# Second layer of a feature-crossing kernel: four more weight tiles as split products, first-layer products moved from VectorE to GpSimd, replicated x1 read from PSUM

## The reference, cut to what matters

```python
def _cin_layer(h, h0, W, b):            # W: (128, Hn*32)
    Wr = W.reshape(128, h.shape[1], 32)
    x = jnp.einsum('bhd,bmd,ohm->bod', h, h0, Wr) + b[None, :, None]
    return relu(x)
x1 = _cin_layer(e, e, W1, b1)           # 32 x 32 products per (b, d)
x2 = _cin_layer(x1[:, :64], e, W2, b2)  # 64 x 32 products per (b, d)
z = sum over d of concat([x1[:, 64:], x2], axis=1)
y = relu(relu(concat([z, dense_ctx]) @ W_top1 + b_top1) @ W_top2 + b_top2) @ W_top3
```

## Time and profile before

| | |
|---|---|
| median of 3 runs | 2141.46 us (2140.15 to 2145.08) |
| the profiled execution's own time | 2145.8 us |
| its span in the trace | 2144.1 us |
| busy in the span: TensorE, VectorE, ScalarE, GpSimd | 98%, 96%, 60%, 54% |
| TensorE clock granted | 0.997 of full speed |
| first product of the second layer on TensorE | at 54.69 us |

### The profile page before, as it was taken

The page is one execution under the profiler, slowest core; times in us unless marked ns, Lnnn a source line. Parts: engine busy times, 40 slices in busy tenths (PEclk is TensorE's granted clock), DMA queues, the critical chain, the costliest instruction groups (busy, mean ns, idle before and its releaser), DMA issues.

```text
span 2144.1 us, 27590 instructions
## 1 busy us (share of the span) xinstructions
PE 2103.7 (98%) x6378; PEld 1204.2 (56%) x6378; DVE 2054.1 (96%) x668; ACT 1285.4 (60%) x4499; POOL 1160.0 (54%) x456
## 2 busy tenths in 40 slices
PE   3999999999999999999999999999999999999999
PEld 1555555555555556555555556555555555555554
DVE  5999999999999999999999999999999999999991
ACT  2565665665665665665665665665665665666653
POOL 4666766666766666677676666666766700000000
PEclk9999999999999999999999999999999999999999
DMA  5676676676676776776776776776676776666650
GB/s 180 192 201 195 193 204 193 198 202 194 202 198 193 205 197 192 204 199 191 204 200 190 205 197 191 205 200 190 199 203 190 202 194 176 186 191 176 184 148 0
DMA packets 226937, 405.59 MB, mean 189 GB/s; under 512 B 33377, under 2 KB 33889, under 8 KB 226802
## 3 DMA queue, kind: packets, MB, share of 16 engines
q1 hardware_dynamic: 212594, 380.32, 61.7%
q0 software_dynamic: 14336, 25.19, 4.6%
HBM read 321.49 MB, written 16.78 MB: 158 GB/s over the span
## 4 chain that ended last, share of the span: by engine, by line
PE 94%; DVE 3%; DMA 2%; issue 1%; SPq 0%; POOL 0%; ACT 0%; DVEq 0%; POOLq 0%; ACTq 0%
PE acc L459 40%; PE acc L453 20%; PE acc L467 10%; PE acc L466 10%; PE acc L471 10%; PE acc L454 1%; DVE pfar L390 1%; DVE pnear L390 1%; DMA x1rep<-x 1%; PE acc L511 0%; PE tp L511 0%; DMA near<-emb_rows 0%; DMA rem_b<-emb_rows 0%; POOL gathered L215 0%; SPq L240 0%
## 5 line engine op out<-in xcount | busy, mean ns | idle before, releaser
L215 POOL DMA_INDIRECT gathered<-in_tables,idx x256 | 933.5, 3646 | 112.4 <-issue 58.5
L459 PE MATMUL acc<-pfar,w2T 128*128 128x512 f32 x2048 | 904.8, 595 | 10.6 <-DVE pfar L390 10.6
L567 ACT CAST phi<-pnear 128x4096 fp32r<-128x4096 f32 x128 | 463.4, 3620 | 541.2 <-DVE pnear L390 301.1
L459 PEld LDWEIGHTS acc<-pfar,w2T 128*128 128x128 f32 x2048 | 389.0, 191 | 481.8 <-issue 468.8
L527 ACT ACTIVATE acc<-acc,bias 128x64 f32<-128x64 f32 (+1 forms) x2048 | 579.7, 286 | 18.8 <-PE acc L471 12.2
L390 DVE TENSOR_TENSOR pnear<-near,x1rep 128x4096 f32<-128x4096 f32 x128 | 566.4, 4425 | 21.0 <-DMA x1rep<-x 17.5
L407 DVE TENSOR_TENSOR plo<-pnear,phi 128x4096 fp32r<-128x4096 f32 x128 | 565.5, 4418 | 0.5 <-ACT phi L567 0.5
L390 DVE TENSOR_TENSOR pfar<-far,x1rep 128x4096 f32<-128x4096 f32 x128 | 565.5, 4418 | 0.0
L453 PE MATMUL acc<-prod,w1T 128*128 128x512 f32 x1024 | 464.9, 597 | 14.7 <-DVE rem_parts L380 12.4
L466 PE MATMUL acc<-phi,w2lo 128*128 128x512 f32 x1024 | 452.8, 442 | 0.0
L527 ACT ACTIVATION_READ_ACCUMULATOR acc<-acc,bias (+2 forms) x2048 | 423.8, 207 | 1.5
(11 more groups left out here) (63 smaller groups left out, 282.8 us busy)
## 6 DMA issues: line engine op xcount, KB each, us to landing
near<-emb_rows SPq DMA_DIRECT2D x512, 256.0 KB, 3.8
far<-emb_rows SPq DMA_DIRECT2D x512, 256.0 KB, 4.4
x1rep<-x SPq DMA_DIRECT2D x256, 256.0 KB, 4.2
h<-emb_rows SPq DMA_DIRECT2D x128, 256.0 KB, 3.2
emb_rows<-gathered POOLq DMA_DIRECT2D x128, 128.0 KB, 3.8
gathered<-in_tables,idx POOLq DMA_INDIRECT x256, 6.5
rem_a<-emb_rows SPq DMA_DIRECT2D x64, 64.0 KB, 3.4
rem_b<-emb_rows SPq DMA_DIRECT2D x64, 64.0 KB, 3.3
```

The source lines that it names most:

```text
L215: nc.gpsimd.indirect_dma_start(out=gathered[:, g, :], out_offset=None, in_=a["tables"], in_offset=bass.IndirectOffsetOnAxis(ap=idx[:, g:g ...
L459: mm = nc.tensor.matmul(acc2[s][:, :], w2T[:, t, :], pfar[:, t // K2, t % K2, :], start=(t == 0), stop=False)
L567: nc.scalar.copy(phi[:, :, :], pnear[:, :, :, :].rearrange("p a k n -> p (a k) n")).then_inc(hi_ready, 1)
```

## The change

- VectorE's products read x1 from PSUM: the replication DMA still writes `x1rep` (now one buffer in SBUF), and ScalarE copies it into `x1p` (two PSUM buffers of 1024 columns).
- `prod1`, `rem_prod` and the remainder's low part move to GpSimd, except those of the start. `prod1` is made for chunk c+2 in step c, so the first layer runs two chunks ahead. `near` gets a third buffer.
- 12 of the 16 second-layer tiles are split: the 8 near ones and the first half of the far ones. 4 stay whole.
- The stores of gathered rows move from GpSimd's queue to SyncE's, with three buffers of `gathered` and `idx`. Two gathers are started in each step.
- The rounding and the low part of the four new split tiles are operations of their own (`phi` and `plo` have 12 tiles).
- The order on TensorE is: high products of the near tiles, first layer of chunk c+2, whole products, low products, high products of the four far tiles.
- The loop has six chunks a turn (19 turns), with 6 written out ahead and 8 behind.

```diff
-x1rep = [sb(f"x1rep_{s}", [P, A2, N]) for s in range(2)]
+x1rep = sb("x1rep", [P, A2, N])
+x1p = [ps(f"x1p_{s}", [P, A2 * N]) for s in range(2)]
 GpSimd, step c:
+                if not odd and within(at, 2):
+                    pool.wait_ge(rem_in, 32 * pair + 64)
+                    pool.wait_ge(rem_lo_ready, pair + 1)
+                    nc.gpsimd.tensor_tensor(rem_prod[:, :], rem_a[:, :], rem_b[:, :], ALU.mult).then_inc(rem_prod_ready, 1)
+                if within(at, 2):
+                    pool.wait_ge(acc1_ready, c + 2)
+                    pool.wait_ge(near_in[(u + 2) % 3], LOADS * (turn * (U // 3)) + LOADS * ((u + 2) // 3 + 1))
+                    nc.gpsimd.tensor_tensor(prod1[:, :, :], near[(u + 2) % 3][:, :, :],
+                                            h0[odd][:, :].unsqueeze(1).to_broadcast([P, K1, N]), ALU.mult
+                                            ).then_inc(p1_ready, 1)
+                if not odd and within(at, 2):
+                    pool.wait_ge(rem_hi_ready, pair + 2)
+                    pool.wait_ge(p1_ready, c + 3)
+                    nc.gpsimd.tensor_tensor(rem_parts[2 * REM:3 * REM, :], rem_prod[:, :], ...).then_inc(rem_lo_ready, 1)
+                    pool.wait_ge(rem_lo_ready, pair + 2)
+                if within(at, 7 - odd):
+                    if not odd:
+                        pool.wait_ge(emb_stored, STORES * pair + STORES)
+                        place_idx(pair + 3, u // 2)
+                    for g in range(2 * odd, 2 * odd + 2):
+                        gather(g, u // 2)
 VectorE, step c:
+                dve.wait_ge(x1p_ready, c + 1)
+                products2(pnear[:, :, :, :], near[u % 3][:, :, :], odd, K1).then_inc(pnear_ready, 1)
+                    dve.wait_ge(lo_far_ready, c)
+                    dve.wait_ge(far_used, c)
+                products2(pfar[:, :, :, :], far[odd][:, :, :], odd, K2).then_inc(pfar_ready, 1)
+                dve.wait_ge(hi_near_ready, c + 1)
+                low(slice(0, T_NEAR), pnear[:, :, :, :]).then_inc(lo_near_ready, 1)
+                dve.wait_ge(hi_far_ready, c + 1)
+                low(slice(T_NEAR, T_SPLIT), pfar[:, 0:1, :, :]).then_inc(lo_far_ready, 1)
 TensorE, step c:
+                pe.wait_ge(hi_near_ready, c + 1)
+                high(odd, range(0, T_NEAR)).then_inc(hi_near_used, 1)
+                    pe.wait_ge(p1_ready, c + 3)
+                    layer1(odd)
+                pe.wait_ge(pfar_ready, c + 1)
+                whole(odd).then_inc(far_used, 1)
+                pe.wait_ge(lo_near_ready, c + 1)
+                low(odd, range(0, T_NEAR))
+                pe.wait_ge(lo_far_ready, c + 1)
+                low(odd, range(T_NEAR, T_SPLIT)).then_inc(lo_used, 1)
+                pe.wait_ge(hi_far_ready, c + 1)
+                high(odd, range(T_NEAR, T_SPLIT)).then_inc(acc2_ready, 1)
 SyncE, step c: replicate_x1 (waits x1_ready, x1p_ready), load_rem of c+3 in odd steps,
   load_near of c+3 (waits pnear_ready, p1_ready), load_far of c+2, store_rows in even steps
 ScalarE, step c: hidden1 of c+1, remainder_hi in even steps, phi of the near tiles,
   copy of x1rep to x1p for c+1, phi of the four far tiles, direct2 of c-1, direct1 of c+1
```

More of the change, by code:

```diff
@@ L189, in software_pipeline, with within, begun @@
         def software_pipeline(eng, step):
[L190 to L196, removed]
+            for c in range(U):
+                step(c, 0, c, c)
+            turns = CHUNKS // U - 1
+            with eng.Fori(1, turns) as turn:
+                for u in range(U):
+                    step(turn * U + u, turn, u, None)
+            for c in range(turns * U, CHUNKS):
+                step(c, c // U, c % U, c)
+        def within(at, ahead):
+            return at is None or at + ahead < CHUNKS
+        def begun(at):
+            return at is None or at > 0
         block = ctx.enter_context(nc.Block())
@@ L391, in products2 @@
                     out, h0part.unsqueeze(1).to_broadcast([P, A2, k, N]),
[L392 to L412, removed]
-                    done = products1(pair + 1, s)
-                    if s == 0:
-                        done = remainder_lo(pair + 1)
-                    done.then_inc(p1_ready, 1)
@@ L474, in _, with high @@
-            pe.wait_ge(p1_ready, 1)
-            layer1(0)
-            def step(c, pair, s, first, last):
-                if not (first and s == 0):
-                    layer2_near(c - 1, 1 - s)
-                if not (last and s == 1):
-                    pe.wait_ge(p1_ready, c + 2)
-                    if not (first and s == 0):
-                        pe.wait_ge(z1_ready, c)
-                    layer1(1 - s)
-                if not first:
-                    pe.wait_ge(z2_ready, c - 1)
-                pe.wait_ge(pfar_ready, c + 1)
-                layer2_far(s)
+            def high(s, parts):
+                for t in parts:
+                    nc.tensor.matmul(acc2[s][:, :], w2lo[:, t, :], phi[:, t, :], start=(t == 0), stop=False)
+                    mm = nc.tensor.matmul(acc2[s][:, :], w2hi[:, t, :], phi[:, t, :], start=False, stop=(t == T_SPLIT - 1))
+                return mm
@@ new lines, in low, with whole @@
+            def low(s, parts):
+                for t in parts:
+                    mm = nc.tensor.matmul(acc2[s][:, :], w2hi[:, t, :], plo[:, t, :], start=False, stop=False)
+                return mm
+            def whole(s):
+                for k in range(K2):
+                    mm = nc.tensor.matmul(acc2[s][:, :], w2T[:, k, :], pfar[:, 1, k, :], start=False, stop=False)
+                return mm
+            pe.wait_ge(rem_lo_ready, 1)
+            for c in range(2):
+                pe.wait_ge(p1_ready, c + 1)
+                layer1(c)
@@ L560, in _, with copy_x1rep @@
             direct1(0, 0)
[L562 to L579 removed]
+            def copy_x1rep(s):
+                nc.scalar.copy(x1p[s][:, :], x1rep[:, :, :].rearrange("p a n -> p (a n)")).then_inc(x1p_ready, 1)
```

268 lines of the change are left out of this document (154 added, 114 removed).

## The result

The changed kernel takes 2060.12 us (median of 4 runs, 2058.09 to 2060.97) against 2140.81 for the kernel before (2139.52 to 2145.08; the table ahead of the prediction has three of these four runs). The ratio is 0.9619, with a 95% interval of 0.9607 to 0.9631. The forecast was 2060.

What follows compares the result with a forecast made beforehand. TensorE was taken to set the pace, VectorE about 0.1 us a chunk behind. (16.04 - 15.42) x 128 = 79 us, and 3 at the end, gave 2064; the median's 4.3 us less gave 2060 us, range 2044 to 2126.

Steps and rivals of the forecast that it cites:

- The main term: TensorE in the loop: four tiles go from whole to fp32r passes, 0.68 us less a chunk, 15.36 in place of 16.04.
- the collision: GpSimd's rem_prod in odd steps reaches 0.4 to 1.3 us into the place of VectorE's near low part.
- VectorE's 15.3: VectorE per chunk: loses prod1 and the remainder (2.97 us), gains a low part (2.3), PSUM operands costing next to nothing.
- the 5.1 that I took: GpSimd's two-input product of 2048 elements: bounds 1.7 to 5.1 us, the upper one taken.
- The third rival: PSUM operands don't free the port for GpSimd products, VectorE is held: 21.7 us a chunk, 2865 us; chance 0.08.
- The fourth rival: GpSimd itself becomes the bound, its gathers shut out as often as before: 15.9 us a chunk, 2120 us; chance 0.06.
- The charge of 0.06 us a chunk: Added to TensorE's 15.36 us for rem_prod meeting VectorE's low part, between 0 and 0.14.
- the self-correction: A late VectorE makes TensorE wait, so GpSimd starts at the early end and rem_prod reaches less into the low part.
- The fifth rival: The longer loop costs a code fetch of 4.2 us at each of 19 branches: 80 us, 2140 us; chance 0.05.
- The end: From last pnear to tower: 19.7 us in place of 23.1, a gain of 3 us.
- The start: Same first loads, ScalarE's copy (about 1 us) added before the first product: nothing either way.
- My schedule: Timing in a chunk: if TensorE waits for VectorE, the first layer ends and prod1 may start at 0, with pnear.

Runs made afterwards that it cites:

- without the collision: Changed kernel with rem_prod made on GpSimd ahead of the gathers and its load issued ahead of the replication of x1: 2055.2 us, ratio 0.9596.
- the kernel with the tiny rem_prod: Changed kernel with rem_prod on GpSimd made for one column of 512 only, in the loop: 2056.4 us, ratio 0.9604.

## Why the prediction was right

*The pace.* The main term is shown. The forecast floor of 15.36 us for TensorE is the measured pace of 15.358 (15.353 without the collision), a whole pass and an fp32r pass cost what the earlier trace rows gave, and adding three passes back gives 16.040, against 16.046 for the kernel before. VectorE's 15.3 is 15.20: reading x1 from PSUM costs nothing (4.41 us), and the new low part 2.20 from start to start.

*GpSimd.* The product took 4.58 us, inside the bounds of 1.7 to 5.1 and near the 4.5 that the Trainium skill gives for an addition of that length ("GPSIMD Engine Reference", "Performance versus the Vector engine"); the 5.1 that I took was 0.5 too much. A remainder operation took 1.30, as charged. The PSUM operand does free the port; the third rival, 2865 us, is near what the kernel becomes with the operand in SBUF: 2736. The fourth rival is out, since gathers fell to 1.85 us and GpSimd is idle for a third of the loop.

*The collision.* Right in place, direction and order of size: the low part is lengthened by 0.32 us per pair on average. The charge of 0.06 us a chunk was too high by a factor of ten (0.005 measured), for TensorE covers it. And the self-correction was overstated: with TensorE waiting, the collision shrinks to 0.1 us a chunk and does not vanish.

*ScalarE and the longer loop.* The busy share that the prediction starts from is misread: 310.8 us over 31.2 chunks is 10.0 us a chunk, not 9.7, so its sum should have been 12.9 and not 12.6. Measured are 12.7 (412.46 of 500 us at 15.36 a chunk). The fifth rival is out as a cost of 80 us; what is seen of it on VectorE is a few tenths of a microsecond at some turns, and that only with 12 chunks a turn.

*The number.* Three errors cancel. First, the loop. Four of the 128 chunks fill the pipeline and don't run at the pace: from the fourth pnear (97.91 before, 99.17 after) to the last (2087.63, 2003.43) there are 124 steps, which give 1989.72 - 1904.26 = 85.5 us, 0.689 each. The prediction had 0.62 x 128 = 79, 6 us too little; the charge of 0.06 for the collision alone is 7. Second, start and end were to give 3 and gave 0.3. Third, the prediction took off 4.3 us more, because the profiled execution before was that much above its median; the changed kernel's profiled execution (2060.19) stands at its median. 85.5 + 0.3 is the 85.7 between the spans, where 82 was forecast.

*The end.* It fell from 23.1 to 21.5 us, not to 19.7. The path was as forecast (TensorE waits for the last phi, then runs its 44 passes), but the clock was left out. After a wait of 2.84 us TensorE starts on the high passes at 2011.54, and from 2012.8 to 2016.3 its granted clock is 0.51:

```profile
2011.54 0.50 PE L523 MATMUL acc<-phi,w2lo 128*128 128x512 f32 x1 [2.84 <-ACT phi L651]
...
2016.91 3.59 PE L534 MATMUL acc<-pfar,w2T 128*128 128x512 f32 x8
```

```profile
2012.80:2016.30 3.50, 3.50 (x10) 2.72 (x9) 3.50 (x1) 3.48 (x16) 0.00 (x0) 0.51 0.00 0
```

That is the lower of its two levels, 1.2 GHz. Passes start 0.43 us apart there and 0.23 before and after, and the 16 high passes take 5.37 us in place of the forecast 3.7. The same stretch of the kernel with the tiny rem_prod ran at 1.00 throughout after a wait of 2.85 us, and its end took 19.9 us, which is the forecast.

*The start.* It lost 1.3 us. In this execution GpSimd's first product held the first low part for 2.7 us, and pfar of the second chunk waited 2.8 us for TensorE, whose first layer ran in part at the lower clock (5.37 us for 3.67). The fourth pnear stands anywhere from 95.6 to 99.2 us in the changed kernel and in those edits of it that keep its pace within a microsecond, so a start is known to some 4 us only. So 2060 is not evidence of a precision of a microsecond: 5 us is what the parts were good for.

## What to carry to other kernels

Two engines at 98% and 96% are one bound: work out both sums per turn of the loop before moving load from one to the other, since relieving VectorE alone gave nothing here, and the passes saved on TensorE with VectorE's load raised made it 8% slower. Where two engines are that close, don't trust the chain for which of them is the bound: shorten one at a time. GpSimd can take a two-input product at half of VectorE's speed without costing it anything, if VectorE's operations beside it have one operand in PSUM; put GpSimd's short two-input operations in that window too, for one that meets a VectorE operation with both inputs in SBUF can cost it nearly its own length (1.07 of 1.33 us above). A collision is free as long as the other engine's sum is longer, so measure it with that engine shortened. A tail that makes TensorE wait can also run at the lower clock: 1.7 us here.

## What the runs showed of the hardware that was not expected

- An operation of GpSimd that is shut out during one low part gets the port at the boundary, ahead of the next low part, although VectorE goes on without an idle gap: 5.33 us for an operation of 1.3, and the next low part 3.35 for 2.28.
- prod1 begins 0.3 to 0.6 us after pnear even when TensorE waits for VectorE (with one whole product less: 999.52 after 999.23, 1015.05 after 1014.42). My schedule let the first layer end with its last pass of 0.229 us, while the row of that product lasts 0.80 us. That this is the whole delay isn't shown.
- Loop bodies of 6 and 12 chunks are fetched again (104 and 121 packets for 4). ScalarE idles for 1.2 to 1.9 us and for 1.7 to 2.9 us at the start of a turn, and only pieces of 2.6 us and more are followed by a wait of VectorE, of 0.2 to 0.3 us.
- TensorE's clock fell to the lower level for 3.5 us at the end of the changed kernel (granted clock 0.51), after 2.84 us without work. In the run with the tiny rem_prod the same wait was followed by 1.00, so the same gap can go either way.
